# Cross attention and a gated recurrent layer on one core: the rounded halves of eight weight chunks by GpSimd's transfers in place of ScalarE's copies

## What is computed

```
q = layernorm(x)                                  # keys and values are the context itself
scores = q k^T * scale, masked to |i - j| <= 64, 16 heads of 32
x1 = x + softmax(scores) v @ W_proj.T + b_proj
x2 = layernorm(x1)
c = in_c
for b in range(8):                                # the recurrence runs over the first axis
    f = sigmoid(x2[b] @ wf.T + c @ uf.T + bf)
    i = sigmoid(x2[b] @ wi.T + c @ ui.T + bi)
    g = tanh   (x2[b] @ wc.T + c @ uc.T + bc)
    c = f * c + i * g
out = x1 + tanh(x2 @ wo.T + c @ uo.T + bo)
```

## Time and profile before

| what | number |
|---|---|
| median of three runs | 942.4 us (942.02 to 944.3) |
| profiled execution, span from first to last instruction | 941.8 us; the page gives no time of its own for this execution |
| the median stands above the span by | 0.6 us |
| TensorE (PE) busy | 918.6 us, 98% |
| VectorE (DVE) busy | 676.1 us, 72% |
| ScalarE (ACT) busy | 476.5 us, 51% |
| GpSimd (POOL) busy | 204.8 us, 22% |
| DMA queues | one queue of transfers issued by SyncE, one by ScalarE; none by GpSimd |
| chain that ended last | PE 85%, DVE 6%, issue 3%, ACT 2%, DMA 2%, POOL 1% |

### The profile page before, as it was taken

One profiled execution on the slowest core, in us unless ns is written; L12 is line 12 of the kernel. 1 busy time (PEld: TensorE's weight loads), 2 busy tenths in 40 slices (PEclk: granted clock), 3 DMA queues, 4 the chain that ended last, 5 costly groups with the idle time before them and its releaser, 6 DMA issues.

```text
span 941.8 us, 21981 instructions
## 1 busy us (share of the span) xinstructions
PE 918.6 (98%) x7842; PEld 715.5 (76%) x7842; DVE 676.1 (72%) x2281; ACT 476.5 (51%) x1430; POOL 204.8 (22%) x228
## 2 busy tenths in 40 slices
PE   7999999899999999999999999999999999999998
PEld 5555567678877788887887888788877888878887
DVE  6888898788779977998799878987798531143222
ACT  6888666655455544645565555555655321131222
POOL 5475322211101111111111111111101100003444
PEclk9999999999999999999999999999999999999999
DMA  9464232234444453544443444433333150059862
GB/s 305 161 192 150 88 96 69 87 89 126 135 111 134 119 143 96 135 110 124 130 141 112 121 114 122 115 107 110 97 98 91 50 163 0 1 179 382 307 237 101
DMA packets 139348, 123.58 MB, mean 131 GB/s; under 512 B 46824, under 2 KB 104168, under 8 KB 137704
## 3 DMA queue, kind: packets, MB, share of 16 engines
q1 hardware_dynamic: 138520, 121.91, 42.6%
q10 hardware_dynamic: 720, 0.27, 0.2%
HBM read 87.70 MB, written 34.46 MB: 130 GB/s over the span
## 4 chain that ended last, share of the span: by engine, by line
PE 85%; DVE 6%; issue 3%; ACT 2%; DMA 2%; POOL 1%; SPq 0%; DVEq 0%; ACTq 0%; POOLq 0%
PE ps_g L684 18%; PE ps_g L686 17%; PE ps_g L685 17%; PE ps_a L731 5%; PE ps_a L753 4%; PE ps_m L684 3%; PE ps_v L774 3%; PE ps_m L686 3%; PE ps_m L685 3%; PE ps_m L806 2%; PE ps_a L684 2%; PE ps_v L779 2%; DVE probs L1013 2%; PE ps_a L686 2%; PE ps_a L685 2%
## 5 line engine op out<-in xcount | busy, mean ns | idle before, releaser
L901 ACT ACTIVATE probs<-probs,rowmin 128x192 f32<-128x192 f32 (+1 forms) x512 | 239.4, 470 | 114.3 <-DVE rowmin L1013 114.3
L1013 DVE CUSTOM_DVE_ANT_0 probs<-ps_a,mask 128x192 f32<-128x192 f32 (+1 forms) x512 | 166.1, 386 | 31.7 <-PE ps_a L731 30.6
L684 PE MATMUL ps_g<-state_hi,gate_w 128*128 128x512 f32 x336 | 133.6, 398 | 0.0
L686 PE MATMUL ps_g<-state_hi,gate_w 128*128 128x512 f32 x336 | 131.1, 390 | 0.0
L685 PE MATMUL ps_g<-state_lo,gate_w 128*128 128x512 f32 x336 | 130.9, 389 | 0.0
L1048 DVE STREAM_TRANSPOSE keys<-probs 32x128 f32<-32x128 f32 x420 | 125.6, 299 | 5.2
L948 ACT ACTIVATE gate<-ps_g,bias 128x512 f32<-128x512 f32 x84 | 57.6, 686 | 105.7 <-PE ps_g L686 105.2
L901 ACT ACTIVATION_READ_ACCUMULATOR probs<-probs,rowmin 128x1 f32 x512 | 96.3, 188 | 0.0
L663 POOL TENSOR_TENSOR attn_lo<-recip,attn_hi 128x512 fp32r<-128x512 f32 x23 | 29.8, 1294 | 276.8 <-ACT attn_hi L914 276.8
L906 ACT ACTIVATE probs_t<-ps_a 128x512 f32<-128x512 f32 x108 | 59.3, 595 | 52.3 <-PE ps_a L753 52.3
L684 PE MATMUL ps_g<-x2t_even,gate_w 128*128 128x512 f32 x192 | 80.0, 417 | 0.0
(11 more groups left out here) (211 smaller groups left out, 1722.4 us busy)
## 6 DMA issues: line engine op xcount, KB each, us to landing
values<-ctx_rows SPq DMA_DIRECT2D x34, 256.0 KB, 4.3
xr<-x SPq DMA_DIRECT2D x32, 256.0 KB, 3.8
keys<-ctx_t SPq DMA_DIRECT2D x16, 512.0 KB, 4.2
x_dram<-xr SPq DMA_DIRECT2D x32, 256.0 KB, 2.6
gate_w<-x2t_dram SPq DMA_DIRECT2D x8, 1024.0 KB, 9.8
keys<-ctx_t SPq DMA_DIRECT2D x16, 384.0 KB, 3.4
x2t_dram<-x2t_even SPq DMA_DIRECT2D x12, 512.0 KB, 4.1
x2t_dram<-x2t_odd SPq DMA_DIRECT2D x12, 512.0 KB, 4.4
```

The source lines that it names most:

```text
L684: pe.matmul(ps, lhs[0], rhs[0], start=start, stop=False)
L686: return pe.matmul(ps, lhs[1], rhs[0], start=False, stop=stop)
L901: act.activation(row, row, ACT.Exp, bias=rowmin[:, i % 2, h:h + 1], scale=-1.0, accum_out=rowsum[:, i // G % 2, i % G, h:h + 1]).then_inc( ...
L1013: dve.tensor_tensor_reduce(probs[:, i % 2, h, 0:SEEN[t]], ps_a[h][:, score_at[i]:score_at[i] + SEEN[t]], mask[:, MASK0[t]:MASK0[t] + SEEN[ ...
```

## The change

The eight chunks 4 to 11 (`ROUNDED`) get their rounded half in another way. A new step `round_w` is put in the list at slots 3, 4, 5, 7, 9, 10, 11 and 13, ahead of the slot's other steps of this kind. In it GpSimd issues a transfer of the chunk from DRAM into the hi part of `gate_w`; source float32, destination float32r. ScalarE's 16 copies of these chunks are gone. GpSimd's subtractions of such a chunk wait for both transfers of it (`w_rounded`, `w_in`), no longer for `w_hi`. The loads of the raw chunks stay where they were.

```diff
@@ -156,6 +156,8 @@
     SPLIT_AT = {1: [0], 2: [1], G: [2, 3], 2 * G: [4, 5, 6], 3 * G: [7, 8, 9], 4 * G: [10, 11]}
+    ROUNDED = range(4, NCH)
+    ROUND_AT = {3: [4], 4: [5], 5: [6], 7: [7], 9: [8], 10: [9], 11: [10], 13: [11]}
@@ -238,6 +240,7 @@
         steps.extend(("load_w", c) for c in LOAD_AT.get(n, [])[:2])
+        steps.extend(("round_w", c) for c in ROUND_AT.get(n, []))
@@ -423,6 +426,7 @@
         w_in = [sem(f"w_in{c}") for c in range(NCH)]
+        w_rounded = {c: sem(f"w_rounded{c}") for c in ROUNDED}
@@ -646,10 +650,19 @@
+                if kind == "round_w":
+                    gt, u, k = chunks[i]
+                    rows = (u_gates if u else w_gates)[gt][k * P:(k + PAIR) * P, :]
+                    pool.dma_start(gate_w[:, gt, u, 0, k:k + PAIR, :], rows.rearrange("(k p) n -> p k n", p=P))\
+                        .then_inc(w_rounded[i], DMA)
                 if kind == "rest":
                     gt, u, k0 = chunks[i]
+                    if i in ROUNDED:
+                        pool.wait_ge(w_rounded[i], DMA)
+                        pool.wait_ge(w_in[i], DMA)
                     for k in range(k0, k0 + PAIR):
-                        pool.wait_ge(w_hi, PAIR * i + k - k0 + 1)
+                        if i not in ROUNDED:
+                            pool.wait_ge(w_hi, PAIR * i + k - k0 + 1)
@@ -930,7 +943,7 @@
-                if kind == "split":
+                if kind == "split" and i not in ROUNDED:
```

## The result

Twenty runs of each kernel: the changed one has a median of 945.19 us, the one before 943.12, and the ratio is 1.002 (95% interval 1.0012 to 1.0028). The change costs 2.1 us by the medians, and 1.1 to 2.6 us by the interval. That is within the 0.3% that was called the same, and on the slow side of it, as forecast; the range, 942.0 to 951.3, held it. Of the 1.2 us between the forecast of 944.0 and the median, 0.7 come from the kernel before: its median was 942.4 in three runs and is 943.12 in twenty.

What follows compares the result with a forecast made beforehand. TensorE was taken to bound the kernel, with GpSimd the bound for some 8 us from 46.5 to 59.5 us. Terms -0 + 1.28 + 0.36 = +1.64 us on the 942.4 median gave 944.0 us, range 942.0 to 951.3.

Steps and rivals of the forecast that it cites:

- The bound: From 46.5 to 59.5 us, GpSimd's subtractions and copy of reciprocals bound the kernel for some 8 us; elsewhere TensorE.
- ScalarE's copies, 0: Removing 16 ScalarE copies, 8.61 us in three bursts beside TensorE's projection, gains 0; ScalarE's busy time falls at least 8.61.
- The price of an issue, c = 1.28 us: Each transfer issue holds GpSimd for c, taken as 1.28 us, one pass over 128x512; bounds 0.43 and 2.69.
- Chunk 9 counts in full: Its issue, ahead of the subtractions at 53.82, meets no GpSimd wait, so TensorE slips by all of c, 1.28 us.
- Chunk 8 counts c - 0.92: Its issue, between 49.50 and 50.42, is partly covered by GpSimd's 0.92 us wait for VectorE; 0.36 us counts.
- the case called nearly free: Rival: c below 0.92, only chunk 9 counts, 0.43 to 0.92 us, time 942.8 to 943.3; chance 0.13.
- Chunks 4 to 7, 10, 11 and the waits on `w_rounded`, 0: GpSimd's waits or VectorE's earlier work cover these issues, and transfers land before subtractions need them; cost 0.
- the hole ahead of chunk 6's subtractions: Sign: GpSimd's order of time shows a gap of c there, near 1.3 us, else the forecast's size is wrong.
- The stretch behind 150 us: Sign: it keeps its length; if it gets longer or shorter, the forecast is wrong in kind.
- The long issue: Rival: GpSimd becomes the bound of the first 92 us; with c = 2.69, 8.9 us, time 951.3; chance 0.27.
- VectorE's hold: Rival: each issue waits for a VectorE normalisation, c 2.37, price 7.0 us, time 949.4; chance 0.07.
- the late landing: Rival: transfers take 15 us to land, chunk 9 is late by some 2 us, time 946 to 948; chance 0.05.

Runs made afterwards that it cites:

- e3: The kernel before, with chunk 6's two subtractions moved from ahead of the copy of reciprocals at 56.3 us to behind it; median 942.08 us, ratio 0.9992.
- e9: The kernel before, with two 128x128 GpSimd additions ahead of chunk 6's subtractions and no transfer by GpSimd; ratio 1.0025.
- e1: The changed kernel, with the transfers of chunks 8, 9 and 11 moved to slots 6, 8 and 12, where GpSimd waits for VectorE; ratio 1.0006.
- e8: The kernel before, with only chunk 9's rounded half by GpSimd's transfer, in slot 10, and the other eleven chunks by ScalarE; ratio 1.0015.
- e2: The changed kernel, transfers at their slots, with the subtractions of chunks 4 to 8 earlier and 9 to 11 following; 942.13 us, ratio 0.999.
- e5: The kernel before, with 12 idle TensorE transposes of the identity ahead of the third turn of reciprocals; ratio 0.999.
- e6: The changed kernel, with chunk 9's transfer issued as two, one for each 128x512 block; ratio 1.0028.

## Why the prediction was right, and where it was not

- **The bound.** Right: GpSimd's chain into the third turn. e3 takes it away, and TensorE's wait goes and the median falls by 1.4 us, with an interval that just includes 1; e9 lengthens it without a transfer and gets the change's time.
- **ScalarE's copies, 0.** Right: e1 makes none of the 16 and has the time of the kernel before. ScalarE's busy time fell by 8.5 us (476.5 to 468.0), 0.1 less than the sign that was named.
- **The price of an issue, c = 1.28 us.** Too high: 0.73 to 0.77 us, and 0.89 for the first. It was inside the bounds of 0.43 and 2.69. The row it was taken from, one pass over 128x512, was the wrong neighbour; GpSimd's single column, 0.55 us, would have been nearer. The Trainium skill's 1 us ("DMA: Bandwidth & Descriptors", latency and other measured facts) is for something else, the first byte, and as a price for the issue the trace has a quarter less.
- **Chunk 9 counts in full.** Right: 0.79 us in the profile, 0.88 in e8.
- **Chunk 8 counts c - 0.92.** The term was right and is 0 at 0.75. The sum of the slip was therefore 0.8, not 1.64: by its own terms the forecast should have been about 943.2, the case called nearly free, to which I had given 0.13.
- **Chunks 4 to 7, 10, 11 and the waits on `w_rounded`, 0.** Right, as far as it can be told: e8, with chunk 9 alone, has a price that can't be told from that of all eight. The transfers landed in 4.6 to 8.5 us, some longer than SyncE's 6.4, but inside the 12 us.
- **What was missing: TensorE's clock.** The text said that the rest of the kernel keeps its length. It doesn't: a wait of 1.92 us in place of 1.16 raised the runs with a fall of the clock from 18 of 88 (other chips among them) to 15 of 20, and in the profiled one the fall cost 1.54 us, twice the slip. An estimate for the mean run: 0.79 for the slip, 0.55 x 1.54 = 0.85 for the runs that now have a fall, and 0.25 x 1.54 = 0.39 for the 5 of 20 that have a second one, together 2.0, where the medians differ by 2.1 and the means by 1.9.
- So the forecast of 1.6 us came near the measured 2.1 by luck, by two errors that cancel: a slip twice too large, and a second term left out. Two of the signs that were named in advance told it: the hole ahead of chunk 6's subtractions is 0.76, not near 1.3; TensorE waits 1.92, not 2.8. The other two, chunk 6's subtractions near 55.5 (55.58) and the turn near 58.2 (58.37), look right only because this execution was 0.98 us late from its start.
- **The stretch behind 150 us** was to keep its length, or the forecast was wrong in kind. From the last turn in this stretch (90.64, 93.93) to the end of the span it is 0.7 us shorter after the change, by the shorter wait for keys; as that wait differs from profile to profile, this sign tells nothing here.
- **The 0.6 us between median and span** is no overhead. In every run that lists both, the time stands 1.75 to 2.0 us above the span, so the profiled execution of the kernel before took some 943.6 us, more than the median of the three runs. The forecast added a difference to the median and is not touched.
- **Rivals.** The long issue, VectorE's hold and the late landing did not happen. On VectorE's hold: the issues at 50.40 and 54.80 took 0.75 and 0.76 us beside VectorE's work, and none of the eight was longer than 0.89, so nothing like the 3.1 us that the Trainium skill has for such a transfer beside a copy ("SBUF — State Buffer", SBUF: two separate sides) was met here. It wasn't tested either: beside the eight issues VectorE ran statistics, reciprocals, score rows, additions with one operand in PSUM and copies out of PSUM (one at 26.21, with an issue of 0.73 us at 26.25), and no copy between two SBUF tiles. The prediction's reading for this rival was also off: both normalisations that it compares, 0.66 us at 51.83 and 1.09 at 67.52, ran beside GpSimd's subtractions. What speaks for a hold is the median over all 32 normalisations, 0.55 us.

## What to carry to other kernels

Before work is given to an engine with 22% busy time, look at the stretch where it is given: GpSimd was the bound for 8 us, and the one issue of the eight that stood there without a wait to hide in was the whole slip. The cure is the same as for any item in that queue, to move it, or what follows it, to where the engine waits anyway. And cost a longer wait of TensorE twice: for its length, and for the clock behind it, which a single profile may or may not show, but the mean clock of many runs does. Take from that the falls that the kernel has anyway, here 2 runs in 10.

## What the runs showed of the hardware

- An issue of a 256-row transfer with a conversion from float32 to float32r, 2 KB a row, holds GpSimd for 0.71 to 0.77 us (0.88 to 0.89 for the first one of a program, in all six kernels that have one), one of 128 rows for 0.54 to 0.61; SyncE's smallest issue of a chunk in the earlier trace rows was 0.43. The transfers landed in 4.6 to 8.5 us beside other traffic, with 512 KB each.
- The share of executions with a fall of TensorE's clock by its wait at this place: none, 6 of 35 (e2, e3, e5); 1.16 us, 18 of 88; 1.51 us, 2 of 12; 1.87 us, 7 of 12; 1.92 us, 15 of 20; 2.04 us, 10 of 12; 2.29 us, 11 of 12. Filled up to 0.47 us with idle transposes, 4 of 12. The falls at no wait come from other waits, such as the 1.20 us near 120 us. The six falls in the profiles (changed, e6, e8, and three in e9) were to half speed and lasted 3.4 us each, apart from those behind TensorE's last work.
- Between executions the start can differ by 1 us ahead of any difference in the program: the same transposes near 6.2 us took 0.66 us in five of the profiles and 0.94 to 1.12 in the six others, and the first turn of reciprocals stands at 21.81 to 22.93. Two spans differ by this without any change.
